# Four-network GNN on one core: attention passes read turned one-hots from DRAM, take the maxima to the edges ahead of the sums, and read leaky message and weights from PSUM

## What is computed

```python
# GIN layer l
msg = relu(h_in[src] + edge_attr_16 @ We[l] + be[l])
agg = segment_sum(msg, dst)
# GATv2 layer, H heads (4, 4, 1)
xl, xr = x @ Wl + bl, x @ Wr + br
m = xl[src] + xr[dst] + edge_attr_32 @ We
m = where(m > 0, m, 0.2 * m)                  # leaky message
s = einsum('ehc,hc->eh', m, att)              # score of an edge
smax = segment_max(s, dst)
ex = exp(s - smax[dst])                       # weight of an edge
out = segment_sum(xl[src] * ex, dst) / segment_sum(ex, dst)
```

## Time and profile before

| | us |
|---|---|
| median of 3 runs | 9243.11 |
| lowest and highest | 9234.94, 9247.55 |
| profiled execution, device time | 9219.24 |
| its span, first to last instruction | 9217.5 |
| mean granted TensorE clock | 0.850 |

### The profile page before, as it was taken

One profiled execution on the slowest core, in us unless ns is written; L12 is line 12 of the kernel. 1 busy time (PEld: TensorE's weight loads), 2 busy tenths in 40 slices (PEclk: granted clock), 3 DMA queues, 4 the chain that ended last, 5 costly groups with the idle time before them and its releaser, 6 DMA issues. The chain is left out here.

```text
span 9217.5 us, 193606 instructions
## 1 busy us (share of the span) xinstructions
PE 7449.7 (81%) x49006; PEld 5555.5 (60%) x49144; DVE 5620.6 (61%) x15108; ACT 3460.9 (38%) x9545; POOL 5315.7 (58%) x5412
## 2 busy tenths in 40 slices
PE   4999888996666656666666689999899999799997
PEld 2444445984444434443444478888688888688886
DVE  5888884013333333333333378888888788778888
ACT  1000002201111211111111167777767677667676
POOL 0001111004777677776777667778588777577774
PEclk9999999997677767677677779999899899789998
DMA  1000014861222222222222222222122222122221
GB/s 44 14 21 29 36 43 176 326 240 47 59 59 60 55 59 59 60 60 55 59 59 60 51 56 59 57 56 59 49 60 59 56 57 58 48 56 57 56 56 42
DMA packets 372827, 615.26 MB, mean 67 GB/s; under 512 B 114410, under 2 KB 277569, under 8 KB 355988
## 3 DMA queue, kind: packets, MB, share of 16 engines
q0 software_dynamic: 150528, 308.58, 12.9%
q1 hardware_dynamic: 221460, 296.64, 9.3%
HBM read 509.70 MB, written 94.96 MB: 66 GB/s over the span
## 5 line engine op out<-in xcount | busy, mean ns | idle before, releaser
L518 POOL DMA_INDIRECT rows_and_onehots<-node_table,idx x4704 | 5001.3, 1063 | 1365.6 <-issue 1217.3
L745 PEld LDWEIGHTS ps<-rows_and_onehots,w 128*128 128x128 f32 x5280 | 1028.7, 281 | 1748.4 <-issue 1705.4
L745 PE MATMUL ps<-rows_and_onehots,w 128*128 128x128 f32 x5280 | 1094.6, 375 | 1122.8 <-issue 1087.0
L1163 DVE TENSOR_TENSOR w<-rows_and_onehots,ps 128x512 f32<-128x512 f32 x663 | 455.7, 687 | 1745.7 <-POOLq L529 1377.8
L639 ACT ACTIVATE w<-w 128x512 f32<-128x512 f32 x663 | 417.3, 629 | 2616.1 <-DVE w L1163 2616.1
L839 PE MATMUL ps<-w_L_conv_edge,ea 65*128 65x512 f32 x1326 | 969.8, 824 | 31.1 <-DMA ea<-in_ea 25.4
L695 ACT ACTIVATE hr<-iota_d,dloc 128x128 f32<-128x128 f32 x2724 | 871.8, 390 | 2.1 <-issue 1.3
L506 POOL TENSOR_TENSOR rows_and_onehots<-rows_and_onehots 128x3210 f32<-128x3210 f32 x25 | 147.0, 5879 | 1254.6 <-ACT rows_and_onehots L602 1254.6
L888 PE MATMUL ps<-w_L_gnn_We,hr 128*128 128x512 f32 x1344 | 827.2, 700 | 31.1 <-issue 28.3
L892 PEld LDWEIGHTS ps<-xrb,hr 128*128 128x128 bf16 x8064 | 571.1, 106 | 452.6 <-issue 452.6
L763 PE MATMUL ps<-w,xrb 128*128 128x512 bf16 (+1 forms) x3026 | 636.6, 366 | 179.1 <-DVE w L1090 175.9
(11 more groups left out here) (221 smaller groups left out, 12246.9 us busy)
## 6 DMA issues: line engine op xcount, KB each, us to landing
rows_and_onehots<-node_table,idx POOLq DMA_INDIRECT x4704
hr<-in_ea SPq DMA_DIRECT2D x672, 64.0 KB
w<-adjacency_turned SPq DMA_DIRECT2D x26, 1600.0 KB, 6.9
adjacency<-rows_and_onehots SPq DMA_DIRECT2D x25, 1600.0 KB, 5.2
w<-adjacency SPq DMA_DIRECT2D x25, 1600.0 KB, 11.2
rows_and_onehots<-adjacency_turned SPq DMA_DIRECT2D x24, 1600.0 KB, 7.1
adjacency_turned<-rows_and_onehots SPq DMA_DIRECT2D x17, 1600.0 KB, 7.0
ea<-in_ea SPq DMA_DIRECT2D x672, 32.0 KB
```

Of the source, the lines that this page charges most:

```text
L518: pool.indirect_dma_start(out=G[q][:, (i % CH) * D:(i % CH + 1) * D], out_offset=None, in_=table[:, :], in_offset=bass.IndirectOffsetOnAxi ...
L745: m = pe.matmul(bank(u % 2, P), rows[u][:, c * D:(c + 1) * D], OH[u][:, c * P:(c + 1) * P], start=(c == 0), stop=(c == CH - 1))
L1163: dve.tensor_tensor(rows[u], Gall[:, bass.ds(at, CH * D)], bank(2 + u % 2), ALU.add).then_inc(S["summed"], 1)
```

## The change

- During GIN pass 0, PE turns each step's f32 one-hots (`OH`) into PSUM banks 4 and 5 right behind the scatter, ACT copies them out in f32 and bf16 (`copy_turned`, one step later), and SP stores both to two new DRAM tensors (256 KB and 128 KB a step).
- In all GAT passes SP loads them back (`OHTB`, `OHT`: two more DMAs a step, four in all), 4 steps deep. Gone are PE's L911, ACT's L699, L686 and L688. SP now waits for the end of the stage before, and before GAT 0 for all stores.
- PE in GAT: the sums of step s-1 (`sum_weighted`) come behind the maxima to the edges of step s; before, the sums of s-1 came ahead of them. `project` waits for `attended`, not `summed`.
- DVE in GAT: `leak` writes its result into the PSUM bank `term[u % 2]`, `attend` reads it there and writes `lk`; `weigh` reads the weights from PSUM bank 0, into which ACT writes them with one more Exp a step.

```diff
+            def store_turned(s, u):
+                row = s * P if isinstance(s, int) else sp.snap(s * P)
+                held(sp, onehots_copied, s + 1)
+                for to, staged in ((onehots32, turned32), (onehots16, turned16)):
+                    sp.dma_start(to[bass.ds(row, P), :], staged[u % 2]).then_inc(onehots_stored[u % 2], 16)
...
                     if "scanned" in S:
-                        held(sp, S["scanned"], s - RING + 1)
-                    parts(g, u)
+                        held(sp, S["scanned"], s - depth + 1)
+                    parts(g, u, s)
+                    if then:
+                        then(s, u)
...
+                def turned_parts(s, u):
+                    if not isinstance(s, int) or s >= 6:
+                        store_turned(s - 6, u - 6)
...
+                begin(sp, f"gat {l} edges")
+                if l == 0:
+                    for i in range(2):
+                        sp.wait_ge(onehots_stored[i], ALL_STORED[i])
...
+                    for of, to in ((onehots16, OHTB[u % 4]), (onehots32, OHT[u])):
+                        sp.dma_start(to, of[bass.ds(s * P, P), :]).then_inc(GAT[l]["edge_data"][u], 16)
-                edge_rows(GAT[l], f"gat {l} edges", RING, gat_parts)
+                edge_rows(GAT[l], f"gat {l} edges", 4, gat_parts)
...
+                def copy_turned(s, u):
+                    act.wait_ge(onehots_turned, s + 1)
+                    held(act, onehots_stored[u % 2], (s - u % 2) * 16)
+                    act.copy(turned32[u % 2], bank(4 + u % 2))
+                    act.copy(turned16[u % 2], bank(4 + u % 2)).then_inc(onehots_copied, 1)
+                def body(s, u, rectify=rectify, copies=l == 0):
+                    rectify(s + 1, (u + 1) % RING)
+                    if copies and on(s - 1):
+                        copy_turned(s - 1, u - 1)
...
+                if l == 0:
+                    copy_turned(STEPS - 1, STEPS - 1)
+                    for i in range(2):
+                        act.wait_ge(onehots_stored[i], ALL_STORED[i])
...
+                        act.activation(bank(0, KH), fall[:, 0:KH], ACT.Exp, scale=-1.0)
                         act.activation(wt[:, :, C], fall[:, 0:KH], ACT.Exp, scale=-1.0).then_inc(S["weight"], 1)
-                    if on(s + 5):
-                        act.wait_ge(S["turned"], s + 6)
-                        act.copy(OHT[(u + 5) % RING], turned)
-                        held(act, S["projected"], s + 4)
-                        act.copy(OHTB[(u + 1) % 2], turned).then_inc(S["onehot_t"], 1)
...
-                    act.activation(OHB[(u + AHEAD) % 2][:, :], far, ACT.Relu, scale=-1.0, bias=1.0)
...
+                    if turns:
+                        held(pe, onehots_copied, s - 1)
+                        for c in range(CH):
+                            m = pe.transpose(bank(4 + u % 2)[:, c * P:(c + 1) * P], OH[u][:, c * P:(c + 1) * P], ident[:, :])
+                        m.then_inc(onehots_turned, 1)
...
-                    held(pe, S["summed"], s - 1)
+                    held(pe, S["attended"], s - 1)
                     pe.matmul(term[u % 2], ea4[u], W[f"L3_gnn_We{l}"][:, :], start=True, stop=False)
-                    pe.wait_ge(S["onehot_t"], s + 1)
...
                         m.then_inc(S["max_of_edge"], 1)
+                    if on(s - 1):
+                        sum_weighted(s - 1, (u - 1) % RING)
...
-                        for c in range(CH):
-                            m = pe.transpose(turned[:, c * P:(c + 1) * P], OHB[(u + 1) % 2][:, c * P:(c + 1) * P],
-                                             identb[:, :])
-                        m.then_inc(S["turned"], 1)
...
-                    dve.scalar_tensor_tensor(out=lk[u % 2], in0=msg[u % 2], scalar=0.2, in1=msg[u % 2], op0=ALU.mult,
+                    dve.scalar_tensor_tensor(out=term[u % 2], in0=msg[u % 2], scalar=0.2, in1=msg[u % 2], op0=ALU.mult,
...
-                    x = lk[u % 2].rearrange("p (c f) -> p c f", f=D)
-                    dve.tensor_tensor(x, x, att[:, None, :].to_broadcast([P, CH, D]), ALU.mult).then_inc(S["attended"], 1)
+                    dve.tensor_tensor(lk[u % 2].rearrange("p (c f) -> p c f", f=D),
+                                      term[u % 2].rearrange("p (c f) -> p c f", f=D), att[:, None, :].to_broadcast([P, CH, D]), ALU.mult).then_inc(S["attended"], 1)
...
-                                      wt[:, :, C:C + 1].to_broadcast([P, KH, C]), ALU.mult).then_inc(S["weighted"], 1)
+                                      bank(0, KH)[:, :, None].to_broadcast([P, KH, C]), ALU.mult).then_inc(S["weighted"], 1)
```

More of the change, by code:

```diff
@@ L190, in build @@
         OH = [arena[:, (RING + i) * CH * P:(RING + i + 1) * CH * P] for i in range(RING)]
-        OHB = [sb(f"OHB{i}", [P, CH * P], BF16) for i in range(2)]
         TOHB = [sb(f"TOHB{i}", [P, CH, TYPES + 1], BF16) for i in range(2)]
@@ L277, in build @@
         summed_up, sums_out = sem("summed_up"), sem("sums_out")
+        onehots_turned, onehots_copied = sem("onehots_turned"), sem("onehots_copied")
+        onehots_stored = [sem(f"onehots_stored{i}") for i in range(2)]
+        ALL_STORED = [32 * (STEPS // 2 + NSG - STEPS), 32 * (STEPS // 2)]
         PARTS = BANKS + 1
@@ L842, in _, with body @@
                 project(0, 0)
-                def body(s, u, S=S, project=project):
+                def body(s, u, S=S, project=project, turns=l == 0):
                     project(s + 1, (u + 1) % RING)
@@ L886, in project, with sum_weighted, body @@
                     pe.wait_ge(S["edge_data"][u], rows_landed(s, u, S))
-                    held(pe, S["summed"], s - 1)
+                    held(pe, S["attended"], s - 1)
                     pe.matmul(term[u % 2], ea4[u], W[f"L3_gnn_We{l}"][:, :], start=True, stop=False)
-                    pe.wait_ge(S["onehot_t"], s + 1)
                     for c in range(CH):
                         for k in range(3):
-                            m = pe.matmul(term[u % 2][:, c * D:(c + 1) * D], OHTB[u % 2][:, c * P:(c + 1) * P],
+                            m = pe.matmul(term[u % 2][:, c * D:(c + 1) * D], OHTB[u % 4][:, c * P:(c + 1) * P],
                                           right[k], start=False, stop=(c == CH - 1 and k == 2))
                     m.then_inc(S["projected"], 1)
-                def body(s, u, S=S, H=H, C=C, KH=KH, project=project):
+                def sum_weighted(s, u, S=S, H=H, C=C):
+                    pe.wait_ge(S["weighted"], s + 1)
+                    held(pe, S["added"], s)
+                    for c in range(CH):
+                        m = pe.matmul(sums, OH[u][:, c * P:(c + 1) * P],
+                                      WT[u % 2][:, c * H * (C + 1):(c + 1) * H * (C + 1)],
+                                      start=(c == 0), stop=(c == CH - 1))
+                    m.then_inc(S["scattered"], 1)
+                def body(s, u, S=S, H=H, C=C, KH=KH, project=project, sum_weighted=sum_weighted):
                     if on(s):
@@ L916, in body @@
                     if on(s + 2):
+                        pe.wait_ge(S["onehot"], s + 3)
                         pe.wait_ge(S["seg_rhs"], s + 3)
@@ L926, in body @@
                         pe.transpose(score_t, score[(u + 3) % 4][:, 0:KH], ident[:, :]).then_inc(S["score_t"], 1)
-                    if on(s):
-                        pe.wait_ge(S["weighted"], s + 1)
-                        held(pe, S["added"], s)
-                        for c in range(CH):
-                            m = pe.matmul(sums, OH[u][:, c * P:(c + 1) * P],
-                                          WT[u % 2][:, c * H * (C + 1):(c + 1) * H * (C + 1)],
-                                          start=(c == 0), stop=(c == CH - 1))
-                        m.then_inc(S["scattered"], 1)
                 walk(pe, body, AHEAD, rounds=13)
+                sum_weighted(STEPS - 1, (STEPS - 1) % RING)
         @block.vector
@@ L1175, in _ @@
                 dve.wait_ge(S["rectified"], STEPS + 1)
+                if l == 0:
+                    dve.wait_ge(onehots_copied, STEPS)
                 dve.wait_ge(S["added"], STEPS)
@@ L1361, in _ @@
                 take_sums(STEPS - 1, (STEPS - 1) % RING)
-                for k, more in (("projected", 4), ("turned", 5), ("onehot_t", 5), ("onehot", AHEAD), ("seg_out", 2),
+                for k, more in (("projected", 4), ("onehot", AHEAD), ("seg_out", 2),
                                 ("score_t", 3), ("scan_back", 2)):
```

33 lines of the change are left out of this document (19 added, 14 removed).

## The result

The changed kernel takes 9153.53 and 9172.35 us against 9245.33 (median of four) of the kernel before on the same chip: a ratio of **0.9914, 95% interval 0.9894 to 0.9933**, some 80 us faster. A second set of runs gave 0.9909. The forecast was 9023, 220 us under the 9243 of before. Two executions of the changed kernel, at 11390 and 12389 us with mean clocks of 0.62 and 0.54, are left out. Ten of the eighteen experiments ran on chips where the kernel before itself took 12.2 to 12.6 ms; every ratio is to the kernel before beside it.

The account below looks back on a forecast made before the run. POOL's gathers, blocked by VectorE's SBUF reads, were taken to stall the GAT passes. From 9219 us, 233 saved there and 13 added in GIN gave 8999 profiled, 9023 as median; own range 8955 to 9095, outer 8900 to 9165.

Parts of the forecast that it names:

- What binds: GAT passes: stalls begin with POOL's gathers, slowed to 1171 ns from 958 beside VectorE instructions with two SBUF inputs.
- The rule put against it: GAT gathers: two SBUF inputs were not seen to stall a software DMA, so PSUM reads would give POOL nothing.
- The price of the PSUM operands: VectorE in GAT: `leak` and `attend` cost 0 to 7 us a pass more, 7 taken; `weigh` nothing.
- Loads and pass starts: GAT one-hot loads stay hidden (3.2 + 3 under 11 us); pass starts change by 0, within 3 us.
- The rival of late loads: GAT: TensorE waits for edge data ahead of the projection, 5.78 us a step, 9449 us in all; chance 0.09.
- GIN pass 0: Added transposes and copies fit idle time; 5 us in late steps and 8 at the end, +13 us.
- Without POOL's holes the lower level should be rare; I leave 18 us a pass: GAT passes: TensorE's time at 1.2 GHz nearly vanishes once POOL keeps pace, leaving 18 us a pass.
- the 373 us of stalls: Three GAT passes: 3656 us less 3283 at 4.93 a step; the most to win beyond shortening the step.
- tile 0: GAT tile 0, 40 groups in a row: POOL at 5.6 us a group still falls behind, 22 us a pass.
- the second wait follows from the first: GAT: VectorE's wait for the projection (40.4 us) comes from POOL's holes, as idle TensorE drops to 1.2 GHz.
- no term of its own: TensorE's maxima ahead of the sums in GAT: nothing new waits, part of the 373 us goes, no separate size.
- leak's block still locks POOL: Rival in GAT: six gathers per two steps remain, only `weigh`'s direct share goes, 93 us, giving 9163; chance 0.18.

Follow-up runs that it names:

- s1: r4's kernel with the leaky message and the weights read from SBUF again: 9274.86 us, 1.0056 of the kernel before.
- r4: Changed kernel with the sums ahead of the maxima again and four unused transposes a step put back on TensorE: 9080.3 us, 0.9831 of the kernel before.
- r2: Changed kernel with the sums ahead of the maxima again, no transposes put back: 9139.12 us, 0.9899 of the kernel before.
- r3: Changed kernel, in its new order, with four unused transposes a step put back ahead of the projection: 9118.48 us, 0.9867 of the kernel before.
- r1: The changed kernel measured once more, nothing altered: 9153.59 us, 0.9909 of the kernel before.
- s2: The kernel before with only the leaky message written to and read from PSUM: 9226.56 us, 0.9994 of the kernel before.

## Why the prediction was wrong

**Right.** *What binds.* POOL's gathers, blocked by VectorE instructions with two SBUF inputs, held up the GAT passes. They came to 1.04 us (forecast 1.0 to 1.08), none is left at 1.19 inside `weigh`, some beside `leak` stay at 1.75, and VectorE's wait for POOL fell to 15.4 us from 121.0. s1 shows it from the other side: without the reads everything of it returns, 1169 ns and 112.8 us. The rule put against it (the Trainium skill, "SBUF — State Buffer", "Who interferes with whom", two SBUF inputs do not stall a software DMA) does not hold here. The same section's sentence that a VectorE instruction with at most one SBUF input, outside the 2-port modes, does not contend with GpSimd agrees with the 0.95 us gather inside L1378.

*The price of the PSUM operands.* Forecast 7 us a pass; L1332 takes 681 ns for 672, L1378 680 for 686, and a step at full clock has a median of 4.92 us for 4.93. It costs nothing that shows in the step.

*Loads and pass starts.* Three waits, of 14.6 us at most, at the heads of the passes, inside stretches that did not grow. The rival of late loads is out. *GIN pass 0:* forecast 13 us, measured 7, with 6.2 of the expected 8 at its end.

**The step that failed** is "Without POOL's holes the lower level should be rare; I leave 18 us a pass". Of the changed kernel's steps, those that meet no lower level are nearly clean: 25 us over 4.93 a step in all three passes, where before they had 117. Those that meet it (in their course or in the 3 us ahead) cost 281 us over 4.93 each, and had cost 256 before. So the 373 us of stalls split into about 117 at full clock, of which 92 went, and 256 around the lower level, which did not fall but rose by 25: 92 - 25 = 67, the gain of the passes. Forecast were 141 us of stalls left (21 for the operands, 66 for tile 0, 54 for the clock); measured are 306, and all but 25 of them lie around the lower level. Two of the prediction's own signs say the same: the GAT clock is 0.89, not above 0.95, and VectorE's idle time before its message addition in pass 0 is 75.9 us, not under half of 105.7.

The reasoning behind it was "the second wait follows from the first": one row showed the lower level behind an idle stretch, and I made it the only way there. It did not follow: VectorE's wait for POOL fell by 105.6 us over the three passes and its wait for the projection rose by 27.2. In the kernel before, too, 20 of the 81 stretches stood behind unbroken busy time. Part of the reasoning holds: with TensorE's stream as before, taking POOL's holes away took the lower level from 600 to 365 us (s1, r4). But I priced the removed transposes and the new order at nothing, "no term of its own", while both change TensorE's stream, and the clock with it. The runs price them: four transposes fewer cost 0.0068 of before in the old order (r4 to r2, 0.9831 to 0.9899, 63 us) and 0.0042 in the new (r3 to r1, 39 us). The new order, with the transposes there, cost 0.0036 (r4 to r3). So once POOL is freed, TensorE's lighter step costs more than it gives: L911's 0.19 us was not "worth nothing" but worth less than nothing. Even r4, with none of this, has 365 us of lower level where I forecast next to none, and reaches 0.9831, 156 us faster than before.

**Missed terms.** The loads and what goes with them (s1) cost 0.0056, 52 us, where the prediction had 0 for the loads and 13 for GIN pass 0. In its profiled execution, the fastest of the six, the passes are 21 us longer than those of the earlier trace rows and the first GAT addition comes 7.6 later; what slows the steps was not found. And by the rivals: the result, 9164 as a forecast by the ratio, lies where "leak's block still locks POOL" put it (9163), but by another cause, for POOL was freed. That the outer range reaches it is luck. The forecast's own range, 8955 to 9095, misses it, and is too narrow for the prices named: halved or doubled all at once, they give 8940 to 9211.

**Open.** That the weights' read alone frees the gathers inside `weigh` is shown by single gathers; that it carries the gain in time is argued from s2 and the blocked kinds, and was not timed alone under the usual condition. What makes the granted clock fall after a fully busy stretch was not found; shown is that the transposes make it rarer in the old order, and not whether by their work or by the moment in the step at which they run. Eight transposes in the new order were not timed under the usual condition.

## What to carry to other kernels

When a change takes work off TensorE in a loop where something else sets the pace, look at the granted clock stretch by stretch before calling it free: here four useless transposes a step took the kernel with the old order from 0.9899 of before to 0.9831. The order of small matmuls belongs to the same look, for it brought drops too. An input moved from SBUF to PSUM can pay on an engine that does not run the instruction: here the gather inside `weigh` went from 1.19 to 0.95 us with one input left in SBUF, and moving `leak`'s output did nothing (s2, 0.9994). Once one stall is removed, ask what was hiding behind it: the same steps were late for POOL and for the clock.

## What was not expected of the hardware

- The granted clock fell to 0.50 behind 5.20 us of 5.20 busy on TensorE by the profile, and was back at 1.00 for the next 5.40. The Trainium skill, "TensorE: Matmul & The Clock Gate", "HAM oscillation — how this bites in real kernels", tells of the drop behind a wait. The traces have both kinds: behind unbroken busy time stand 20 of 81 stretches before the change and 110 of 141 after it.
- Lower-level time in the GAT passes fell 519, 365 (zero and four spare transposes), then 95 us (eight) in one order, at POOL waits of 31.0, 32.3 and 13.1 us.
- On three chips the same kernels ran a third slower, with long waits between engines (POOL for VectorE up to 31.5 us at once), and there the order of the kernels turns: all with a read from PSUM took 1.5 to 5% more than the kernel before, the changed one without those reads 0.5% less, and the kernel before with only the new order 1.2% less. Whether it is the chip or a passing condition was not found.
